# Expert tiles: a gather that waits for the last reader of its ring place, and its row numbers written earlier

## The reference

```
x = x + tanh(g_xattn) * attention(layernorm(x), context)          # before the part of interest
z = layernorm(x)
probs = softmax(z @ gate_w.T + gate_b)                            # 10 gates: 8 experts, 2 that give nothing
weights, selected = top_k(probs, 2)                               # null choices masked, the rest normalised
out = sum over the 2 choices of  weight * (z @ expert_w[e] + expert_b[e])
x = x + tanh(g_ffn) * out
```

## Time and profile before

| | us |
|---|---|
| median of three runs | 1397.64 |
| the profiled execution | 1394.18 |
| its span in the profile | 1392.4 |
| the expert stage, from the first gather at 965.90 to the end | 426.5 |
| TensorE busy in 1200 to 1240 | 38.22 of 40 |

### The profile page before, as it was taken

One profiled execution on the slowest core, in us unless ns is written; L12 is line 12 of the kernel. 1 busy time (PEld: TensorE's weight loads), 2 busy tenths in 40 slices (PEclk: granted clock), 3 DMA queues, 4 the chain that ended last, 5 costly groups with the idle time before them and its releaser, 6 DMA issues. The chain is left out here.

```text
span 1392.4 us, 30166 instructions
## 1 busy us (share of the span) xinstructions
PE 1309.5 (94%) x7339; PEld 671.3 (48%) x7340; DVE 1105.9 (79%) x2797; ACT 752.4 (54%) x2724; POOL 694.2 (50%) x645
## 2 busy tenths in 40 slices
PE   7999999999999999999999999993998988999997
PEld 5434555555555555555555555541544444444443
DVE  6776888998999999999999999885666665666665
ACT  5655666665666666656656665652443333344332
POOL 1501222445545445445545545545666666666664
PEclk9999999999999999999999999996999999999999
DMA  8144788878977878978779877973455435676772
GB/s 306 50 170 128 184 197 185 192 185 225 213 189 182 188 185 227 218 176 190 190 180 244 205 178 180 185 172 115 134 142 142 146 132 187 220 244 214 229 232 100
DMA packets 413298, 256.17 MB, mean 184 GB/s; under 512 B 338979, under 2 KB 350307, under 8 KB 413077
## 3 DMA queue, kind: packets, MB, share of 16 engines
q1 hardware_dynamic: 385365, 180.89, 53.4%
q0 software_dynamic: 27840, 74.18, 16.8%
HBM read 111.61 MB, written 75.01 MB: 134 GB/s over the span
## 5 line engine op out<-in xcount | busy, mean ns | idle before, releaser
L908 PE MATMUL scores<-arena,zT 128*128 (+2 forms) x2304 | 414.8, 338 | 3.4 <-PEq L159 3.4
L1023 ACT ACTIVATE expd<-scores,less 128x77 f32<-128x77 f32 x1024 | 317.4, 328 | 183.0 <-DVE less L1127 181.9
L923 PE MATMUL mix<-u_sb,pT 128*128 128x512 f16 x1728 | 383.5, 379 | 1.3 <-DMA pT<-p_parts 0.7
L1876 PE MATMUL out_bank<-arena,expert_yT 128*128 x1440 | 334.6, 383 | 5.2 <-issue 3.0
L908 PEld LDWEIGHTS scores<-arena,zT 128*128 128x128 f16 x2304 | 220.6, 98 | 170.0 <-issue 5.7
L923 PEld LDWEIGHTS mix<-u_sb,pT 128*128 128x128 f16 x1728 | 169.0, 98 | 198.3 <-issue 0.8
L1876 PEld LDWEIGHTS out_bank<-arena,expert_yT 128*128 128x128 f16 x1440 | 142.0, 99 | 153.2 <-issue 13.2
L1023 ACT ACTIVATION_READ_ACCUMULATOR expd<-scores,less 128x1 f32 x1024 | 213.4, 208 | 0.0
L1597 POOL DMA_INDIRECT table<-payload,row_i x128 | 159.8, 1248 | 60.1 <-issue 35.8
L1901 ACT CAST expert_yT<-yT_bank 128x512 f16<-128x512 f32 x120 | 70.2, 585 | 211.8 <-PE yT_bank L1863 101.6
L1989 DVE SCALAR_TENSOR_TENSOR result<-out_bank,slots,biased 128x512 f32<-128x512 f32 x120 | 90.1, 751 | 101.3 <-remote 51.5
(11 more groups left out here) (183 smaller groups left out, 1669.6 us busy)
## 6 DMA issues: line engine op xcount, KB each, us to landing
comb<-x_out SPq DMA_DIRECT2D x64, 512.0 KB, 3.2
x_ln<-in_x_dram SPq DMA_DIRECT2D x64, 256.0 KB
x_res<-in_x_dram SPq DMA_DIRECT2D x64, 256.0 KB
w_raw<-in_L_ffn_expert_w_dram SPq DMA_DIRECT2D x64, 128.0 KB, 2.3
u_dram<-u_stage SPq DMA_DIRECT2D x12, 512.0 KB, 2.8
u_sb<-u_dram SPq DMA_DIRECT2D x6, 1024.0 KB, 8.0
arena<-in_L_xattn_w_kv_dram SPq DMA_DIRECT2D x4, 1024.0 KB, 7.9
slots<-table SPq DMA_DIRECT2D x150, 2.0 KB
```

Source lines behind the costliest of these rows:

```text
L908: last = pe.matmul(scores[s][k][:, 0:n], zT[:, s, zp, t, :], m, start=(t == 0 and (zp, mp) == PRODUCTS[0]), stop=(t == DT - 1 and (zp, mp) ...
L923: last = pe.matmul(mix[:], pT[:, s, pp, k, :], u_sb[:, k, up, :], start=(k == 0 and (pp, up) == PRODUCTS[0]), stop=False)
L1023: last = act.activation(expd[:, s, h * KEYS:(h + 1) * KEYS], scores[s][k][:, at:at + KEYS], ACT.Exp, bias=less[:, s, h:h + 1], scale=1.0 / ...
L1876: last = pe.matmul(c.out_bank[s][:], yT[:, s, yp, t, :], w_of[:, bass.ds(e, 1), t, wp * D:(wp + 1) * D].rearrange("p a n -> p (a n)"), sta ...
```

## The change

Two edits. A gather waits for `biased_ready` of the tile whose ring place it takes, in place of `result_ready`. And VectorE names the rows of tile j+5 ahead of its three operations for tile j, in place of behind them; without this the gather would still wait for row numbers that come after the result.

```diff
@@ gathers (GpSimd)
                 pool.wait_ge(c.token_ready, (j - EARLY if c.k == 1 else j) + 1)
                 if later(j, R):
-                    pool.wait_ge(c.result_ready, 2 * (j - R) + 2)
+                    pool.wait_ge(c.biased_ready, j - R + 1)
@@ step (VectorE)
                     if live(1):
                         low_y(c, R * r + s + 1, buffer(s + 1))
+                    named = R if c.k == 0 else EARLY
+                    if live(R) and not (first_pass(r) and s + R < named):
+                        name_token(c, *at(r, s, R))
                     if live(0):
                         j = R * r + s
                         name_out(c, r, s, j, tiles)
                         weigh_bias(c, r, s, j, pass_experts[s])
                         finish(c, r, s, j)
-                    named = R if c.k == 0 else EARLY
-                    if live(R) and not (first_pass(r) and s + R < named):
-                        name_token(c, *at(r, s, R))
```

## The result

The changed kernel takes 1402.42 us (median of 9 runs, 1400.76 to 1406.96) against 1397.96 (9 runs, 1394.19 to 1400.95) for the kernel before, three of whose runs are those of its first timing. The ratio is 1.0039 with a 95% interval of 1.0027 to 1.0051, so it is slower: by 4.5 us between the medians, by 5.5 as the ratio has it. The forecast was 3 us faster. The profiled execution took 1401.75 us, 7.57 more than the one before. That one, with 1394.18, was the fastest of its kernel, 3.8 under the median of its runs, so the two profiles differ by more than the kernels do. In the experiments' timings two single executions, of 1972.92 us (wait alone) and 6425.62 us (order alone, second timing), lie far outside all others and are left out of the ratios.

A forecast was written before the change was run, and what follows sets the result against it. TensorE was taken to bound the expert stage. Earlier gathers in choice 1 return 3.0 us of a 4.2 us ceiling, the other terms 0, so 1397.64 - 3.0 = 1394.6 us, range 1390.5 to 1399.0.

The forecast's parts named there:

- The wait of a gather: GpSimd, choice 1: gathers start 1.65 us earlier in an even stretch, 2.0 at the pause, returning 3.0 us on TensorE.
- the sum: Whole kernel: 3.0 us returned by earlier gathers in choice 1, taken off the median of 1397.64, gives 1394.6 us.
- the change touches nothing of it: Expert stage's pauses: TensorE's signals come late whatever the gathers do, so pauses keep their number and length.
- I expect nothing from the 50 tiles of choice 0: Choice 0, where ScalarE waited for gathers only twice, 5.7 us, at the stage's start: no gain expected.
- The rival in which the pauses change: Each of 11 pauses shortens by 0.2 us and more than the bubbles returns: 7 us gained, 1390.6 us; chance 0.27.
- the one rival that ended slower: GpSimd becomes the bound at a cycle of 3.17 us over TensorE's 3.03: 1406.9 us, or 1404; chance 0.11.
- VectorE's order: Row numbers of 0.14 us ahead of biased and result on VectorE: taken as 0, at most 1.5 us gained or lost.
- The scatter and the stretching: GpSimd: scatter can start at 1218.43, before 1220.41; stretching of at most 0.52 us moves from gather to scatter; both 0.
- GpSimd bounds nothing: GpSimd's even cycle is 2.65 us of 3.03, leaving 0.38 for stretching; a scatter pushed back is held shorter.
- The transfers: DMA moves the same data sooner: at best 0, at worst the queue swallows the whole advance, costing the 3.0 us.
- the 8 forecast: Sign in the changed kernel's profile: ScalarE's 26.2 us of waiting for gathers of choice 1 falls below 8.

The follow-up runs named there:

- wait alone: Kernel before with only the gather's wait moved to biased, row numbers still behind the result: ratio 1.0002 (0.9988 to 1.0016), without pauses.
- order alone: Kernel before with only the row numbers moved ahead of biased and result, gather still waiting for the result: ratios 0.9989, 1.0000, 0.9998 without pauses.
- the last timing: Kernel before with only VectorE's row numbers moved ahead, on a chip with pauses: 1394.10 us against 1400.12, ratio 0.9960 (0.9945 to 0.9975).
- the old choice 1: Kernel before with both edits in choice 0 only, so its choice 1 is unchanged; two timings without pauses: ratios 0.9994 and 1.0000.

## Why the prediction was wrong

*The wait of a gather*: right. The earlier trace rows had the gather 1218.71 - 1215.45 = 3.26 us behind the start of biased. In the changed kernel without pauses:

```profile
1217.75 1.01 POOL L1800 DMA_INDIRECT two_ring<-comb,token  x1 [0.30 <-issue]
...
1218.83 0.74 DVE L1964 SCALAR_TENSOR_TENSOR biased<-u_sb,slots,two_ring 128x512 f32<-128x512 f32 x1
1219.07 1.40 POOL L1821 DMA_INDIRECT out_dram<-result,token_out  x1 [0.31 <-DVE token_out L1982]
...
1220.77 1.01 POOL L1800 DMA_INDIRECT two_ring<-comb,token  x1 [0.30 <-issue]
```

It is 1220.77 - 1218.83 = 1.94 there, 1.3 us earlier in place of 1.65, since the scatter in front holds it, not biased. The returned 3.0 us of the sum were 3.5 where no pause disturbs, and where they do the excess behind late gathers fell by 3.0, from 3.93 to 0.93.

*What failed* is the assumption under the sum: "the change touches nothing of it", that is of the late signals, and with it "I expect nothing from the 50 tiles of choice 0". I had seen that the pauses are most of the stage's loss, 28.3 us in 102 tiles, and gave them no term, because neither a gather nor a transfer released them. That nothing in the profile releases a wait does not make it independent of what is moved. Between the two profiles the excess that begins with pauses rose by 5.9 us in choice 0 and 4.8 in choice 1, against 3.0 saved. By an estimate 3 of these 10.7 are there because the profiled execution before was 3.8 under its median and the changed one 0.7 under its own; the rest, less what was saved, is about the 4.5 us between the medians. By what path the change makes the pauses dearer is open. The rival in which the pauses change had the wrong sign, for it let them shorten, and the one rival that ended slower, with a chance of 0.11, had another mechanism.

*VectorE's order*, 0 with 1.5 to both sides: right without pauses (three ratios within 0.0011 of 1), too narrow with them, where it returned 6.0 us in the last timing. Which of its effects gives that is open; the kernel before has no profile on that chip.

*The scatter and the stretching*: right. It moved as forecast: the gathers' maximum of 1532 ns is now

```profile
L1800 POOL DMA_INDIRECT two_ring<-comb,token x66: 986/1007/1388, 1161.8 to 1377.9; - x66
...
L1821 POOL DMA_INDIRECT out_dram<-result,token_out x70: 971/1031/1447, 1164.4 to 1394.8; - x70
```

and the scatters are the longer ones; without pauses their median is 1303 ns, that of the gathers 1008. That GpSimd bounds nothing held too, by the reason given: in the even stretch without pauses its cycle is 1.40 + 0.30 + 1.01 + 0.31 = 3.02 us, as long as TensorE's 3.03, for the stretch adapts: a scatter that starts later is held less. The scatter at 1219.07 lies beside biased for 1219.57 - 1219.07 = 0.50 us and takes 0.39 longer than the 1.01 of its neighbour. The Trainium skill (SBUF — State Buffer, Who interferes with whom) has the later of the two blocked until the first ends. The trace agrees where biased is first, and better than the prediction had it: a scatter that began with 0.50, 0.40, 0.31 or 0.18 us left of biased took 1.40, 1.30, 1.21 or 1.08 us, and 1.03 with none, so its end stays 0.90 behind that of biased. It does not agree the other way round: in the same trace 33 operations that make biased in choice 1 began during a scatter or a gather, and none took over 0.76 us.

*The transfers*: right. They didn't swallow the advance: ScalarE's wait fell to 6.3 us. Without pauses it was 10.2 in the changed kernel, a little over the 8 forecast, against 24.7 and 29.0 with the old choice 1.

## What to carry to other kernels

A wait whose releaser the profile doesn't name belongs in the sum with bounds of both signs, sized by its whole share of the stage, even if the change touches neither end of it. Time a small gain on more than one chip and at more than one time before it is kept: here the same edit was 0.22% faster and 0.39% slower, in intervals of a tenth of a percent. And where two edits are each needed for an effect, neither alone shows it, so a test of the parts must include the pair.

## What was not expected of the hardware

- The program has at least two conditions, with 1361.7 to 1363.0 and about 1400 us for the kernel before; once it took 1379.8. One chip showed both, 23 minutes apart. The granted clock is 1.00 in choice 0 in both. Most of what lies between them goes with the late signals: the kernel before had 32.3 us of excess with them (in 1394.18), and kernels that have only the order or the wait, and run as long as it, had 3.0 to 4.5 without.
- In the late condition two signals of TensorE that belong to different operations arrive together, mostly 1 to 2.8 us behind the end of the transposes (0.4 at least and 3.6 at most), when the multiplications already issued have run out.
- What makes the signals late is open. One trait of the traces is the distance: in the five of them the tile right behind a late signal had another in 46 of 173 cases; else the second had it in 6 of 129, the third in 63 of 122, the fourth in 45 of 60. A second trait goes along with it: behind a pause GpSimd's instructions follow each other every 1.33 us, 2.66 for a tile's two, and so gain 0.37 us a tile on TensorE. Of 72 tiles in which the last of them started 0.65 to 0.85 us before the transposes' end, 36 had the late signal, and 11 of 68 with 0.35 to 0.45 us (tiles behind a late one left out). Over half of the first band are third tiles, so the two can't be told apart. An earlier gather shifts that phase, which could be how it costs time. That was not tested, nor why three tiles are the usual distance.
